# Token attention of a macaron layer: 128-row products on zero-padded queries and weights, with the sum of the weights as a 17th value column

## The reference, cut to what matters

```python
def _L0_ffn_ref(x, gamma1, Wq, bq, Wdown, bdown, Wup, bup, Wo, bo, gamma2, Wg, bg, We):
    h = _rmsnorm(x, gamma1)
    q = (h @ Wq + bq).reshape(b, t, H, HD)                       # H = 16, HD = 16
    kv = ((h @ Wdown + bdown) @ Wup + bup).reshape(b, t, H, 2 * HD)
    k, v = jnp.split(kv, 2, axis=-1)
    att = jnp.einsum('bthd,btgd->bthg', q, k) / np.sqrt(HD).astype(np.float32)
    att = jax.nn.softmax(att, axis=-1)
    out = jnp.einsum('bthg,btgd->bthd', att, v).reshape(b, t, D)
    x = x + (out @ Wo + bo)
    h2 = _rmsnorm(x, gamma2)
    gate = jax.nn.softmax(h2 @ Wg + bg, axis=-1)
    combined = jnp.einsum('btd,edf,bte->btf', h2, We, gate)      # 8 experts
    return x + combined
...
x = x + 0.5 * _L0_ffn_ref(_layernorm(x, axis=-1), ...)
x = x + _L0_attn_ref(_layernorm(x, axis=-1), ...)
x = x + 0.5 * _L0_ffn_ref(_layernorm(x, axis=-1), ...)
```

## Time and profile before

| | |
|---|---|
| median of three runs | 1177.39 us (1176.49 to 1179.04) |
| the profiled execution | 1170.35 us |
| its span, first to last instruction | 1168.3 us |
| PE busy | 1069.3 us, 92% of the span |
| DVE, POOL, ACT busy | 911.8, 735.9, 607.4 us |
| mean granted PE clock | 0.979 of full speed |
| PE records | 15416 MATMUL and 15416 LDWEIGHTS, of 36619 instructions |

### The profile page before, as it was taken

The page is one execution under the profiler, slowest core; times in us unless marked ns, Lnnn a source line. Parts: engine busy times, 40 slices in busy tenths (PEclk is TensorE's granted clock), DMA queues, the critical chain, the costliest instruction groups (busy, mean ns, idle before and its releaser), DMA issues. The chain is left out here.

```text
span 1168.3 us, 36619 instructions
## 1 busy us (share of the span) xinstructions
PE 1069.3 (92%) x15416; PEld 811.3 (69%) x15416; DVE 911.8 (78%) x1467; ACT 607.4 (52%) x1203; POOL 735.9 (63%) x693
## 2 busy tenths in 40 slices
PE   5699999989899989999999999876989899999897
PEld 4587878868688756555656655555878778787785
DVE  7788788777785369999999999977777696885743
ACT  4445345434364457767767776633634354453442
POOL 8757458455473348888888878961856474572534
PEclk9799999999999999999999999989999999999999
DMA  6300000000000000000000000000000000000000
GB/s 186 101 3 2 3 3 1 3 2 2 3 2 2 1 1 2 1 2 2 2 1 2 1 2 2 1 2 3 2 20 1 21 20 3 20 1 21 20 2 37
DMA packets 8442, 14.82 MB, mean 13 GB/s; under 512 B 2516, under 2 KB 6102, under 8 KB 8280
## 3 DMA queue, kind: packets, MB, share of 16 engines
q1 hardware_dynamic: 8280, 12.47, 3.2%
HBM read 8.28 MB, written 4.19 MB: 11 GB/s over the span
## 5 line engine op out<-in xcount | busy, mean ns | idle before, releaser
L439 PE MATMUL psum<-we,h 128*128 128x512 f32 x1536 | 403.5, 406 | 2.7 <-issue 2.7
L439 PEld LDWEIGHTS psum<-we,h 128*128 128x128 f32 x1536 | 279.7, 190 | 65.2 <-issue 3.7
L1405 POOL TENSOR_TENSOR late<-late 128x512 f32<-128x512 f32 x64 | 82.5, 1289 | 231.1 <-ACT late L1234 231.1
L1234 ACT ACTIVATE late<-psum,gate 128x256 f32<-128x256 f32 x256 | 107.1, 471 | 155.0 <-PE psum L439 134.0
L1095 DVE TENSOR_REDUCE oT<-psum 128x128 fp32r<-128x1024 f32 x128 | 155.6, 1218 | 31.4 <-PE psum L797 31.4
L1068 DVE SCALAR_TENSOR_TENSOR X<-psum,gate,X 128x256 f32<-128x256 f32 x256 | 123.0, 481 | 58.8 <-PE psum L439 47.5
L1284 ACT ACTIVATE kvx<-psum 128x1024 f32<-128x1024 f32 x128 | 131.2, 1025 | 70.8 <-PE psum L807 68.2
L1443 POOL TENSOR_TENSOR kvx<-kvx,late 128x2048 f32<-128x2048 f32 x32 | 124.4, 3888 | 35.0 <-ACT late L1291 35.0
L1101 DVE TENSOR_REDUCE late<-kvx 128x256 f32<-128x2048 f32 x64 | 145.7, 2277 | 0.0
L1443 POOL TENSOR_TENSOR late<-kvx,late 128x2048 f32<-128x2048 f32 x32 | 124.8, 3899 | 29.5 <-ACT late L1291 29.5
L807 PE MATMUL psum<-oT,neg_id 128*128 128x512 f32 x256 | 93.8, 447 | 18.0 <-DVE oT L1095 17.5
(11 more groups left out here) (149 smaller groups left out, 2007.0 us busy)
## 6 DMA issues: line engine op xcount, KB each, us to landing
X<-in_L_attn_hidden_states SPq DMA_DIRECT2D x8, 512.0 KB, 5.5
out<-X SPq DMA_DIRECT2D x8, 512.0 KB, 2.6
X<-in_L_ffn_We SPq DMA_DIRECT2D x2, 1024.0 KB, 10.1
kvx<-in_L_ffn_Wq SPq DMA_DIRECT2D x1, 256.0 KB, 2.8
kvx<-in_L_ffn_Wup SPq DMA_DIRECT2D x2, 128.0 KB, 2.6
kvx<-in_L_ffn_Wo SPq DMA_DIRECT2D x1, 256.0 KB, 3.9
X<-in_L_attn_Wk SPq DMA_DIRECT2D x1, 256.0 KB, 2.8
X<-in_L_attn_Wq SPq DMA_DIRECT2D x1, 256.0 KB, 3.1
```

What stands on the lines that cost most here:

```text
L439: ins = e.matmul(out_ap, l, r, start=(n == 0 and not opened), stop=(n == len(terms) - 1), skip_group_check=opened)
L1234: e.activation(y[:, n // 2 * 2 + w, :], psum[:, u % 3, w * D:(w + 1) * D], ACT.Copy, scale=gate[k % 2][:, i, 2 * n + w:2 * n + w + 1]).the ...
L1405: own.step(e.tensor_tensor(y[:, 0:2, :], y[:, 0:2, :], y[:, 2:4, :], ALU.add))
```

## The change

- `windows` is replaced by `token_scores` and `token_values`. Each issues 32 products instead of 64. A product takes all 128 partitions of a row. Its 32 stationary columns are 16 for the upper four tokens and 16 for the lower four, each with zeros on the partitions of the others. It writes the same 32 PSUM partitions, and nothing is added up.
- `qc` becomes two buffers of [128, 32 rows, 2, 16]. `q_turn` writes the second group of 16. A new ACT step `q_up` copies partitions 0 to 63 of it into the first group, and a new POOL step `q_zero` then clears what was copied. `scores` waits for `q_zero`.
- `at` becomes one buffer of that shape. The step `at` is now four copies of 64x256, and waits for `attend` of the pair before.
- The value rows of `kvx` get a 17th column of ones (written by POOL for pairs 0, 1, 16 and 17, which fills both buffers for each ffn block). The product then gives the sum of the weights beside the 16 outputs, and moves 68 columns instead of 64.
- `total` is gone. `mult` now takes the reciprocal of the sums out of PSUM and multiplies in one operation of 128x512. `top` subtracts in one operation of 128x512 instead of two of 128x256.
- `scores` takes one bank of the ring instead of banks 3 and 4.
- DVE's `expand_V` writes runs of 16 instead of single elements 16 apart.
- The output comes out with the tokens in another order, which the transposes of `oT` set right with `swap`, a permuted identity. The experts' gate now shares `ct` with the attention over the sequence, with two waits for it.
- The lengths and needs in `all_steps` follow, so the order of all engines is made anew.

```diff
 def all_steps(B, NT, KC):
...
-            put("PE", 1650, ("q", s, p), ("hT_lo", s, p), ("scores", c - 3), ("split_lo", 1), ("rest_lo", 2))
+            put("PE", 1650, ("q", s, p), ("hT_lo", s, p), ("scores", c - 2), ("split_lo", 1), ("rest_lo", 2))
             put("DVE", 1160, ("q_turn", s, p), ("q", s, p))
+            put("ACT", 620, ("q_up", s, p), ("q_turn", s, p))
+            put("POOL", 450, ("q_zero", s, p), ("q_up", s, p))
...
-            put("PE", 1450, ("attend", c), ("at", c), ("turn_out", c - 1))
-            put("DVE", 800, ("mult", c), ("attend", c), ("total", c))
+            put("PE", 440, ("turn_probs", c), ("exp", c), ("attend", c - 1))
+            put("ACT", 1500, ("at", c), ("turn_probs", c))
+            put("PE", 1200, ("attend", c), ("at", c), ("turn_out", c - 1))
+            put("DVE", 1250, ("mult", c), ("attend", c))
...
-        def windows(e, left, right, w):
+        def token_scores(e, queries_, keys):
 
             for a4 in range(4):
-                for half in range(2):
+                for odd in range(2):
                     for j in range(4):
-                        pi = 4 * a4 + j
-                        for u in range(2):
-                            rows = slice(u * HALF, (u + 1) * HALF)
-                            ins = e.matmul(psum[32 * j:32 * j + 32, 3 + u, a4 * HALF:(a4 + 1) * HALF],
-                                           left[rows, pi, half * H:half * H + 2 * H], right[rows, 2 * pi + half, w, :, :],
-                                           start=(half == 0), stop=(half == 1), skip_group_check=True)
+                        r = 8 * a4 + 2 * j + odd
+                        ins = e.matmul(psum[32 * j:32 * j + 32, keys[0], (2 * a4 + odd) * HALF:(2 * a4 + odd + 1) * HALF],
+                                       queries_[:, r, :, :], keys[1][:, r, 0, :, 0:HD], start=True, stop=True, skip_group_check=True)
+            return ins
+
+        def token_values(e, weights, values):
+
+            for a4 in range(4):
+                for odd in range(2):
+                    for j in range(4):
+                        r = 8 * a4 + 2 * j + odd
+                        n = (a4 % 2 * 2 + odd) * T4 * (HD + 1)
+                        ins = e.matmul(psum[32 * j:32 * j + 32, 3 + a4 // 2, n:n + T4 * (HD + 1)],
+                                       weights[:, r, :, :], values[:, r, 1, :, :], start=True, stop=True, skip_group_check=True)
             return ins
...
 # DVE, "mult" ("total" is gone)
...
+                        e.wait_ge(s_on, c)
                     e.wait_ge(s_attend, c + 1)
...
+                    own.step(e.reciprocal(r_, ps[:, :, :, HD]))
+                    e.wait_ge(own.sem, own.n)
+                    e.tensor_tensor(on.rearrange("p (a t d) -> p a t d", a=2, d=HD), ps[:, :, :, 0:HD],
+                                    r_.unsqueeze(3).to_broadcast([P, 2, NR // 2, HD]), ALU.mult).then_inc(s_on, 1)
...
 # ACT
+                elif name == "q_up":
...
+                    e.wait_ge(s_q_turned, 2 * k + p + 1)
+                    e.activation(qc[p][0:HALF, :, 0, :], qc[p][0:HALF, :, 1, :], ACT.Copy).then_inc(s_q_up, 1)
...
                 elif name == "at":
...
-                    if c >= 2:
-                        e.wait_ge(s_attend, c - 1)
+                    if c:
+                        e.wait_ge(s_attend, c)
+                    else:
+                        e.wait_ge(s_pad, 3)
                     e.wait_ge(s_pT, c + 1)
...
-                    e.activation(dst, src, ACT.Copy).then_inc(s_at, 1)
+                    turned = psum[:, b, :].rearrange("p (m u h) -> p m u h", u=2, h=H)
+                    dst = at[:, :, :, :].rearrange("p (m o) u h -> p m o u h", o=2)
+                    for odd, u in product_of((0, 1), repeat=2):
+                        ins = e.activation(dst[u * HALF:(u + 1) * HALF, :, odd, u, :], turned[odd * HALF:(odd + 1) * HALF, :, u, :], ACT.Copy)
+                    ins.then_inc(s_at, 1)
...
 # POOL
+                elif name == "q_zero":
+                    p = piece[2]
+                    e.wait_ge(s_q_up, 2 * k + p + 1)
+                    e.memset(qc[p][0:HALF, :, 1, :], 0.0).then_inc(s_q_zero, 1)
```

More of the change, by code:

```diff
@@ L1 @@
 from contextlib import ExitStack
+from itertools import product as product_of
 import concourse.bass as bass
@@ L24 @@
         "oT": ("oT_hi", "oT_lo"), "wo": ("x1",), "h2T": ("h2_hi", "h2_lo"), "gate": ("gate_copy",), "gateT": ("gate_sub",),
-        "a_hT": ("a_hT_hi", "a_hT_lo"), "qk": ("part",), "v": ("v_out",)}
-WIDE = {"kv": ("kv_turn",), "scores": ("top",), "attend": ("mult",)}
+        "a_hT": ("a_hT_hi", "a_hT_lo"), "qk": ("part",), "v": ("v_out",), "scores": ("top",)}
+WIDE = {"kv": ("kv_turn",), "attend": ("mult",)}
 TAKEN = RING | WIDE
-BY_JOB = {"stats", "norm", "xs", "hT", "hT_hi", "hT_lo", "down", "la_hi", "la_one", "la_lo", "q", "q_turn",
+BY_JOB = {"stats", "norm", "xs", "hT", "hT_hi", "hT_lo", "down", "la_hi", "la_one", "la_lo", "q", "q_turn", "q_up", "q_zero",
           "kv", "kv_turn", "oT", "oT_hi", "oT_lo", "x1_base", "wo", "x1", "square", "rms2", "half", "xs2", "h2T", "h2_hi", "h2_lo",
           "gate", "gate_copy", "gateT", "gate_sub", "gate_exp", "gate_soft"}
-BY_PAIR = {"expand_V", "expand_P", "expand_A", "scores", "top", "exp", "total", "turn_probs", "at", "attend", "mult", "turn_out", "out_turn"}
+BY_PAIR = {"expand_V", "expand_P", "expand_A", "scores", "top", "exp", "turn_probs", "at", "attend", "mult", "turn_out", "out_turn"}
 def attention_plan(B, NT, KC):
@@ L306, in port @@
     def port(p):
-        return steps[p][0] == "POOL" or p[0] in ("half", "split_lo")
+        return steps[p][0] == "POOL" or p[0] in ("half", "split_lo", "expand_V")
     def possible(p):
@@ L861, in expand @@
                     rows, t4 = slice(n // T4 * NR // 2, (n // T4 + 1) * NR // 2), n % T4
[L862 to L864 removed]
+                    ins = emit(kvx[c % 2][:, rows, :, t4, 0:HD].rearrange("p r w d -> p (r w) d"),
+                               kvc[c % 3][:, rows, :, :].rearrange("p r w d -> p (r w) d"), mask4[:, t4:t4 + 1])
+            if who == "P" and c % (2 * B) < 2:
+                ins = e.tensor_scalar(kvx[c % 2][:, :, 1, :, HD], mask4[:, :].unsqueeze(1).to_broadcast([P, NR, T4]), 1.0, 1.0,
+                                      ALU.mult, ALU.mult)
             ins.then_inc(s_kvx[who], 1)
@@ L1295, in act_program @@
                         e.wait_ge(a_ctT, f)
+                    else:
+                        e.wait_ge(s_gTT, done(B - 1))
                     e.wait_ge(a_values, NT * (f + 1))
```

100 lines of the change are left out of this document (37 added, 63 removed).

## The result

The changed kernel takes **1104.95 us** (median of 4 runs, 1103.58 to 1107.81) against 1176.94 us (4 runs) for the kernel before: a ratio of 0.9389, with a 95% interval from 0.9365 to 0.9412. A later set of runs gave 1105.37 us (6 runs, 1103.21 to 1110.13).

The account below looks back on a forecast made before the run. PE was taken to bound a middle job. From 1170.35 us, 20 for pieces and 21 for pauses and clock came off, 4.4 was added, giving 1133.7; plus 7.0 for the median, rounded to 1140.5 us, range 1126 to 1166 us.

Parts of the forecast that it names:

- shorter pieces: PE's scores and attend pieces fall from 1.42 to 1.03 and 1.08 us; 20 us gained in all.
- pauses inside pieces: Most of PE's 25.8 us of issue waits go: 13 us in the PE-bound stretches, 3 us elsewhere.
- the -4.4: Loss of 4.4 us in all from longer at, mult, q_up and q_zero and places of this kind.
- half clock: Stretches of 3.4 us at half clock behind PE's pauses; three of four counted as going, 5 us.
- The slower rival: Stationary loads no longer hide behind matmuls in scores and attend, a piece takes 2.76 us, total 1236 us; chance 0.06.
- the two stretches that PE bounds: From 62 to 400 us and from 870 us on; their 48 of 64 pieces were counted in full.
- 7.0 us that I added for the median: Median of runs before lay 7.0 us above the profiled one; added to 1133.7 us to give 1140.7 us.
- this counts nothing: DVE's relief put at no gain, as DVE is not on the path in a middle job.
- (c): q_up and q_zero before scores, two-deep qc and single at: 2 us lost, bounds 0 and 8 us.
- (d): DVE loses total, 675 + 353 ns a pair, and waits less in expand_V; counted as nothing.
- the 16 pieces outside of the two stretches: Pieces in the first 62 us and the passage to the second ffn block; counted half, 3 us.
- The share of dense places: Places in PE's order where 256 instructions finish in under 3.3 us; to fall from 14% to under 1%.

Follow-up runs that it names:

- experiment 1: Changed kernel with each scores and attend product cut in two, so a piece has 128 MATMUL records again; 1166.19 us against 1104.95 us.
- experiment 2: Kernel before with half its records, each window's second product left out and the others moving 128 columns; 1128.91 us, ratio 0.9592.
- experiment 6: Changed kernel with only the scores products cut in two, attend keeping 64 records; 1125.93 us, 21.0 us more.
- experiment 5: Changed kernel with DVE's expand_V written as before the change; 1111.32 us, 6.4 us more.
- experiment 7: Changed kernel with four extra copies ahead of the four real ones in every at step on ACT; 1128.07 us, 23.1 us more.

## Why the prediction was wrong

By its own steps, in the profiled executions (span 1168.3 us before and 1101.7 us after, 66.6 us less; forecast 36.6):

| term | forecast | the two traces |
|---|---|---|
| shorter pieces | 20 | 64 x 0.36 = 23.0 |
| pauses inside pieces | 16 | 23.8 |
| "issue" waits ahead of `scores` (for `expand_V`, `q_zero`) | part of the -4.4 | 2.0 - 8.5 = -6.5 |
| "issue" waits at other lines | 0 | 2.9 |
| half clock | 5 | (49 - 22) / 2 = 13.5 at most |
| waits of the product lines for DVE and POOL | 0 | 16.2 - 5.2 = 11.0 |
| `at`, `mult`, `q_up`, `q_zero` | -4.4 | no wait for `at`; `q_zero` counted above |
| other waits of PE | 0 | -2.3 |

The last column adds up to 65.4 us. The last row is PE's wait at lines 439 and 444 for `hT` (4.4 us before, 9.3 us after), those of line 439 for `kvcs` and `top` (3.6 us, gone), and 1.0 us more at `turn_out`, which waits for `mult`.

**Right:** the pieces, to the hundredth (forecast 1.03 and 1.08 us, measured 1.03 and 1.09), and with them the choice of line 823 as the row to go by. The slower rival, loads that no longer hide, is dead. The Trainium skill ("TensorE: Matmul & The Clock Gate", Part 3) lists that LDWEIGHTS overlaps only with matmuls of another row group; the same part also lets a load be pulled ahead when it goes to the background weight buffer. The first statement alone does not hold for this form: 64 loads of 113 ns on all 128 rows would be 7.2 us one after the other, and the piece takes 1.03 us. No run shows whether the weight buffer is what allows it. That the pauses hang on the number of records was right as well, as experiments 1, 2 and 6 show. That they are instructions which have not arrived fits the places of the pauses, and is not shown beyond that. `at` was forecast at 370 to 470 ns a copy and takes 379 ns; it is level with PE's work, as said.

**Wrong, the half clock.** I looked for stretches at 0.50 only behind pauses in the two stretches that PE bounds, found four, and counted three of them, 5 us. The mean clock of the whole span, which was there to be read, said 49 us at the half clock, so up to 25 us. By the trace 14 us of the 49 are the four that I found; 17 us lie in the start (from 28, 38 and 52 us) and 10 us in the passage to the second ffn block (from 762 and 799 us). After the change the four are gone, the start has 10 us instead of 17, one stretch of 3.4 us in the attention is gone too, and the passage still has 10 us. So half of the fall is the term that I had, for which 5 us was too little, and the other half lies where I had not looked. The clock is also behind a part of the 7.0 us that I added for the median: it wanders from run to run (0.971 to 0.985 in 26 runs of the kernel before, with times from 1184 to 1167 us), the profiled execution was one of the better ones, and the changed kernel's median lies only 1.4 us above its profiled one. I carried 7.0 us over as if it were a constant; that is 5.6 us of the 35.6.

**Wrong, "this counts nothing".** Steps (c) and (d) took the bank, DVE's relief and `expand_V` as neutral or small losses, since DVE has 8 us to spare in a middle job. Yet the waits for `kvcs`, `top` and `kvx` stood in the list of waits, 16.2 us, right below the row that I used. Put back one at a time, the bank costs 8.6 us, `total` 7.1 us and the old `expand_V` 6.4 us. They can't simply be added to the 61.2 us of the records: that makes 83 us, more than the 72 us. I take this to be because the order of pieces and the clock answer to each of them, and because the new steps cost something too: the waits ahead of `scores` for `expand_V` and `q_zero` grew by 6.5 us. I had 2 us for places of this kind, with 8 us as the bound.

**Wrong, where pieces and pauses count.** I let the 16 pieces outside of the two stretches count half and the pauses there a third, "since pairs that wait for one another would wait anyway". All 19 pauses inside pieces went, those elsewhere too: 23.8 us where I counted 16. In experiment 1 the records cost 61.2 us where my two terms for them hold 41. By the traces of that kernel and the changed one the 62.6 us between their spans are 23 us of pieces if all 64 count in full, 23.6 us of issue waits at the product lines (29.9 us more inside pieces, 6.3 us less ahead of `scores`), 11 us of clock ((44 - 22) / 2) and 5 us of smaller delays. So the start and the passage, where pairs wait for one another, gave no discount: a late piece there delays what waits for it. The share of dense places, which I put at 14% before the change, is 7.5% when counted by the starts in the trace, and experiment 6 shows that it does not forecast the pauses.

In short, of the 35.6 us about 20 belong to the records' true price and the rest to parts that I had put at +4.4 us and that are worth some 11 us of gain, net of what the new steps cost.

What stays open: what in the chip is late at the place in the packet, why the clock differs from run to run of one kernel, and the operation of 6.7 us on DVE in the start of the changed kernel.

## What to carry to other kernels

When many small instructions are asked of one engine in a short time, count the instructions of a piece as well as its work: merging products so that half the records remain was worth 61 us of 1166 here, of which only 23 us were the pieces themselves. Read the half clock from the mean granted clock of the whole span before looking for single stretches, and read every row of the bounding engine's waits, not only the row that the change aims at. Look also at where in a piece an "issue" wait lies: inside a piece it was a pause of PE's own, ahead of a piece it was a wait for data that the profile did not name. "This engine has time to spare" says little about work that the planner may not place: the same load cost 7 us placed and 20 us unplaced.

## What the runs showed of the hardware

- Pauses of 1 to 3 us in the middle of a PE piece, with all data there, each time at the same place (192 or 193) in a count of 256 PE instructions, in all 32 gaps of over 0.9 us of two kernels. They came with dense pieces: 14 and 18 with 128 records in every piece, 3 with 128 in every other one, none with 64.
- Loads of the stationary data (108 to 114 ns each) hid behind matmuls of 64 columns that use all 128 rows and four places of 32 columns: 64 records and loads took 1.03 us, and line 823, with as much streaming in 16 records, takes 1.00 us. Eight places of 64 rows took 1.09 us with 64 records of 128 columns (experiment 2).
- POOL's `expand_P` fell from 1019 ns to 749 ns an operation, though its own work did not change apart from rows of 17 in the target. With DVE's old writes it takes 805 ns, so some 55 ns of it hang on how DVE writes; the rest of the 270 ns was not tried.
- One operation of `expand_V` on DVE, 0.49 us in the median, took 6.7 us in the start of the changed kernel, in both of its traces and in that of experiment 5 (6.9 us), and each time ended 0.3 to 0.5 us behind four products on POOL. In experiments 1, 6 and 7 the longest one is 1.5 us. The cause was not tried.
- The time of the kernel before differs by up to 17 us (1167 to 1184 us) over 26 runs in three sets; the fastest run had the highest mean granted clock (0.985), the slowest one the lowest (0.971), though not every run in between keeps that order.
